# Selection products of the second attention on 48 rows, in pairs over two row tiles, with one buffer of transposed keys

## What is computed

```python
def _L1_attn_ref(x, w_attn, w_proj):   # H = 16 heads of 8 elements, T = 512
    qkv = x @ w_attn
    q = qkv[..., :D].reshape(Bv, Tv, H, HEAD_D).transpose(0, 2, 1, 3)
    k = qkv[..., D:D + HEAD_D]          # one key and one value for all heads
    v = qkv[..., D + HEAD_D:]
    att = jnp.einsum('bhqd,bkd->bhqk', q, k) * scale
    att = jnp.where(causal[None, None, :, :], att, -jnp.inf)
    att = jax.nn.softmax(att, axis=-1)
    y = jnp.einsum('bhqk,bkd->bhqd', att, v)
```

## Times and profile before

| | us |
|---|---|
| median of three runs | 853.83 (848.96 to 860.17) |
| profiled execution, time | 861.02 |
| its span | 859.3 |
| busy: PE, DVE | 681.4, 583.3 |
| busy: ACT, POOL | 349.4, 328.8 |

### The profile page before, as it was taken

The page is one execution under the profiler, slowest core; times in us unless marked ns, Lnnn a source line. Parts: engine busy times, 40 slices in busy tenths (PEclk is TensorE's granted clock), DMA queues, the critical chain, the costliest instruction groups (busy, mean ns, idle before and its releaser), DMA issues. The chain is left out here.

```text
span 859.3 us, 14978 instructions
## 1 busy us (share of the span) xinstructions
PE 681.4 (79%) x4376; PEld 413.4 (48%) x4409; DVE 583.3 (68%) x1923; ACT 349.4 (41%) x748; POOL 328.8 (38%) x430
## 2 busy tenths in 40 slices
PE   1579989984048999999974779898989898898794
PEld 1445666652025788777762224444444444443353
DVE  8378888886921312544357988888889898977373
ACT  0322333304302212222311127666666666666761
POOL 0256656640065636677630003333333332333330
PEclk9999999997558859999995579999999999999996
DMA  9200000000411212222234213020404040300021
GB/s 297 80 1 1 0 1 0 1 1 26 134 40 32 37 19 35 34 40 38 35 77 55 37 22 49 12 57 3 56 4 56 3 57 9 50 4 3 1 62 38
DMA packets 40350, 32.44 MB, mean 38 GB/s; under 512 B 3608, under 2 KB 36936, under 8 KB 40280
## 3 DMA queue, kind: packets, MB, share of 16 engines
q1 hardware_dynamic: 30448, 23.51, 12.6%
q0 software_dynamic: 7840, 6.86, 5.4%
q10 hardware_dynamic: 1992, 1.21, 0.8%
HBM read 13.60 MB, written 8.13 MB: 25 GB/s over the span
## 5 line engine op out<-in xcount | busy, mean ns | idle before, releaser
L1602 ACT ACTIVATE pexp<-wide 128x512 f32<-128x512 f32 (+2 forms) x384 | 183.7, 543 | 118.5 <-PE wide L1791 112.3
L1551 POOL TENSOR_SCALAR_AFFINE_SELECT pexp<-pexp 128x256 f32<-128x256 f32 x256 | 107.3, 422 | 284.1 <-ACT pexp L1602 282.6
L1414 DVE CUSTOM_DVE_ANT_0 masked<-bank,mask_qk 128x384 f32<-128x384 f32 (+3 forms) x356 | 155.2, 480 | 22.0 <-PE bank L1742 20.0
L1791 PE MATMUL wide<-qT,kTe 128*128 128x256 bf16 (+3 forms) x501 | 120.7, 301 | 19.0 <-ACT pexp L1602 8.8
L1070 ACT ACTIVATE hT<-wide,b1T 128x512 f32<-128x512 f32 x64 | 43.5, 687 | 162.8 <-PE wide L1090 134.3
L1742 PE MATMUL bank<-kTm,qT 128*128 128x384 bf16 (+3 forms) x348 | 89.0, 320 | 17.1 <-DVE mx L1414 8.7
L1804 PE MATMUL bank<-pexp,vx 128*32 128x512 f32 (+3 forms) x1024 | 95.5, 445 | 0.8 <-POOL pexp L1551 0.8
L945 POOL DMA_INDIRECT x_dram<-yg,row_u x40 | 63.9, 1596 | 58.0 <-DVE yg L994 49.5
L1414 DVE CUSTOM_DVE_ANT_0 masked<-wide,mask_qk 128x256 f32<-128x256 f32 (+3 forms) x156 | 74.3, 499 | 15.5 <-PE wide L1742 12.9
L938 POOL DMA_INDIRECT x_row<-xln_dram,row_u x64 | 61.8, 965 | 52.8 <-DVE slot_tok L815 33.6
L1099 PE MATMUL bank<-w_sb,hT 128*128 128x128 f32 x512 | 75.4, 292 | 3.2 <-issue 3.2
(11 more groups left out here) (232 smaller groups left out, 1071.8 us busy)
## 6 DMA issues: line engine op xcount, KB each, us to landing
qT<-qp SPq DMA_DIRECT2D x135, 64.0 KB
x_sb<-in_L_attn_x SPq DMA_DIRECT2D x8, 256.0 KB, 6.7
w_sb<-in_L_ffn_w SPq DMA_DIRECT2D x1, 2048.0 KB, 13.1
xln_dram<-rx SPq DMA_DIRECT2D x8, 256.0 KB, 2.3
out_x<-x_sb SPq DMA_DIRECT2D x8, 256.0 KB, 2.3
x_dram<-x_sb SPq DMA_DIRECT2D x5, 256.0 KB, 3.5
x_sb<-x_dram SPq DMA_DIRECT2D x5, 256.0 KB, 3.0
x_row<-xln_dram,row_u POOLq DMA_INDIRECT x64
```

The costliest lines, as they stand in the source:

```text
L1414: ins = nc.vector.tensor_tensor_reduce(out=masked[:, n % 4, at], in0=bank_of(n)[:, at], in1=mask_qk[:, T - w:T], scale=1.0, scalar=LEAST, ...
L1551: nc.gpsimd.affine_select(out=pexp[:, n % 4, :, 0:P], in_=pexp[:, n % 4, :, 0:P], pattern=[[0, 2], [1, P]], compare_op=ALU.is_ge, fill=0.0 ...
L1602: nc.scalar.activation(pexp[:, (2 * step + h // 2) % 4, h % 2:h % 2 + nh, 0:w], psE[m % 3][:, 0:nh * w].rearrange("p (h t) -> p h t", h=nh ...
L1791: ins = nc.tensor.matmul(psE[m % 3][:, hh * w:(hh + 1) * w], kTe[:, par, j * P:(j + 1) * P], qT[:, b % QB, 4 * qd + h + hh, j * P:T], star ...
```

## The change

1. The max products keep the six largest pairs of parts, 48 rows. Heads 0 to 7 have them in rows 0 to 47, heads 8 to 15 in rows 64 to 111; the three remaining pairs lie in other rows (`ROWS_OF_HALF`), and `KEYS_IN_BLOCKS` fills the key slots to fit, with four DVE copies in place of three. The scores products still sum all nine pairs, now over 123 rows (`QR` is 120).
2. `pe_max_pair` makes a unit of a lower and of an upper head together: matmuls on rows 0 to 47 and on rows 64 to 111 alternate, into two banks. It waits for both banks and for the rows of both halves.
3. Units are numbered in pairs, and `PAIRS_IN_STEP` places pairs: the first of a step in place B, the second in D (step 12: C).
4. `kTe` and its copy go; `kTm` has three buffers and the rows of -1 (120 to 122), set once by POOL at the start of the kernel.

```diff
+    BLOCKS = 2 * P // 16 - 1
+    QR = BLOCKS * L
+    LARGE = 6 * L
+    ROWS_OF_HALF = (((0, 3, 5), (1, 4, 6), (2, 7, 14)), ((8, 11, 13), (9, 12, 6), (10, 7, 14)))
+    KEYS_IN_BLOCKS = ((0, 0, 2, 0, 3), (1, 0, 2, 3, 5), (1, 0, 1, 7, 8), (2, 0, 2, 5, 7))
...
-        kTm = sb("kTm", [P, 2, T], BF16)
+        kTm = sb("kTm", [P, QB, T], BF16)
...
-        for h0 in range(0, HEADS, 4):
+        for h0 in range(0, HEADS // 2, 4):
             for k in range(NT):
                 nh = max(1, 4 // (k + 1) if k != 2 else 1)
-                max_units += [(k, h, nh) for h in range(h0, h0 + 4, nh)]
+                for h in range(h0, h0 + 4, nh):
+                    max_units += [(k, h, nh), (k, h + HEADS // 2, nh)]
...
-        IN_STEP = (4, 3, 2, 2, 1, 2, 2, 2, 5, 4, 3, 3, 2, 4, 2, 3)
-        AHEAD = sum(IN_STEP[SHIFT_STEP:])
+        PAIRS_IN_STEP = (2, 2, 1, 1, 1, 1, 1, 0, 2, 2, 2, 1, 1, 1, 2, 2)
+        AHEAD = 2 * sum(PAIRS_IN_STEP[SHIFT_STEP:])
...
-                n = 0 if spot not in spots else IN_STEP[s] // len(spots) + (spots.index(spot) < IN_STEP[s] % len(spots))
+                n = 2 * (spot in spots[:PAIRS_IN_STEP[s]])
...
-            return ops(kx3[:, :, :, n, :], kp[:, n].unsqueeze(2).broadcast_to([P, NT, PARTS, L]))
+            part, g0, ng, lo, hi = KEYS_IN_BLOCKS[n]
+            return ops(kx3[:, :, g0:g0 + ng, lo % 8:lo % 8 + hi - lo, :],
+                       kp[:, part].unsqueeze(2).unsqueeze(2).broadcast_to([P, NT, ng, hi - lo, L]))
...
-        def dve_kTe(dve, b, par):
-            dve.wait_ge(q_kTm.sem, q_kTm.at(b, 1))
-            if b:
-                dve.wait_ge(q_sp.sem, q_sp.at(b - 1, 0))
-            nc.vector.tensor_copy(kTe[0:QR, par, :], kTm[0:QR, par, :]).then_inc(q_kTe.sem, 1)
...
-            nc.vector.memset(vx[:, :, :, :], 0.0)
-            nc.vector.tensor_copy(kTe[64:P, :, :], shift_rows[64:P, :].unsqueeze(2).broadcast_to([64, 2, T])).then_inc(q_init.sem, 1)
+            nc.vector.memset(vx[:, :, :, :], 0.0).then_inc(q_init.sem, 1)
...
-                for j in range(PARTS):
-                    row = (n * PARTS + j) * L
+                for block in ROWS_OF_HALF[half][n]:
+                    row = block * L
...
-        def pe_max_unit(pe, b, n, place):
+        def pe_max_pair(pe, b, n, places):
+
             k, h, nh = max_units[n]
-            pe.wait_ge(q_row[h // 8].sem, q_row[h // 8].at(b, PARTS * PARTS))
+            for half in range(2):
+                pe.wait_ge(q_row[half].sem, q_row[half].at(b, PARTS * PARTS))
             pe.wait_ge(q_kTm.sem, q_kTm.at(b, 1))
             w = P * (k + 1)
             for hh in range(nh):
-                ins = nc.tensor.matmul(place[:, hh * w:(hh + 1) * w], qT[:, b % QB, h + hh, k * P:(k + 1) * P],
-                                       kTm[:, b % 2, 0:w], start=True, stop=True)
-            ins.then_inc(q_smp.sem, 1)
+                for half, place in enumerate(places):
+                    rows = slice(64 * half, 64 * half + LARGE)
+                    ins = nc.tensor.matmul(place[:, hh * w:(hh + 1) * w],
+                                           qT[rows, b % QB, 8 * half + h + hh, k * P:(k + 1) * P],
+                                           kTm[rows, b % QB, 0:w], start=True, stop=True)
+                    if hh == nh - 1:
+                        ins.then_inc(q_smp.sem, 1)
...
+            pool.wait_ge(s_c.sem, s_c.total(16))
+            nc.gpsimd.tensor_copy(kTm[96:P, :, :], const("shift_rows")[96:P, :].unsqueeze(2).broadcast_to([P - 96, QB, T])).then_inc(s_zero.sem, 1)
+            pool.wait_ge(s_zero.sem, s_zero.total(3))
```

More of the change, by code:

```diff
@@ L1229, in build @@
         vx = scratch("vx", [P, 2, NT, 32])
-        kx3 = scratch("kx3", [P, NT, PARTS, PARTS, L], BF16)
-        kTe = scratch("kTe", [P, 2, T], BF16)
+        kx3 = scratch("kx3", [P, NT, 2, 8, L], BF16)
         mx = scratch("mx", [P, NT, HEADS])
@@ L1381, in dve_k_slots @@
             dve.wait_ge(q_kTp.sem, q_kTp.at(b, 0))
-            for n in range(PARTS):
+            for n in range(len(KEYS_IN_BLOCKS)):
                 fill_k_slots(nc.vector.tensor_copy, n).then_inc(q_kx.sem, 1)
@@ L1465, in dve_turn @@
                         dve_divide(dve, b - 1, tail_of(b).divide[s, place])
-                    if middle and s == KTE_STEP and place == "A":
-                        dve_kTe(dve, b + 1, 1 - b % 2)
+                    if middle and s == V_STEP and place == "A":
                         dve_v(dve, b + 1, 1 - b % 2)
@@ L1585, in act_kv, with act_kT @@
                                  ACT.Copy).then_inc(q_kv.sem, 1)
-        def act_kT(act, b, par):
+        def act_kT(act, b):
             act.wait_ge(q_kTp.sem, q_kTp.at(b, 1))
-            act.wait_ge(q_smp.sem, q_smp.at(b - 1, 0))
-            act.wait_ge(q_kTe.sem, q_kTe.at(b - 1, 0))
-            nc.scalar.activation(kTm[0:QR, par, :], psA[:, :].bitcast(BF16)[0:QR, 0:T], ACT.Copy).then_inc(q_kTm.sem, 1)
+            if b >= QB:
+                act.wait_ge(q_sp.sem, q_sp.at(b - QB, NS))
+            nc.scalar.activation(kTm[0:QR, b % QB, :], psA[:, :].bitcast(BF16)[0:QR, 0:T], ACT.Copy).then_inc(q_kTm.sem, 1)
         def act_exp(act, b, step, parts=None):
@@ L1640, in act_turn @@
                 if front and s == KT_STEP:
-                    act_kT(act, b + 2, b % 2)
+                    act_kT(act, b + 2)
         def mqa_act(act):
@@ L1690, in mqa_sync @@
         def mqa_sync(sp):
-            sp.wait_ge(s_zero.sem, s_zero.total(2))
+            sp.wait_ge(s_zero.sem, s_zero.total(3))
             q_rows(sp, 0, 0)
@@ L1759, in pe_max @@
                     pe.wait_ge(q_kTm.sem, q_kTm.at(b + 1, 1))
-                pe_max_unit(pe, b, n, bank[i])
+                if n % 2:
+                    pe_max_pair(pe, b, n - 1, (bank[unit_bank[n - 1]], bank[i]))
         def pe_max_at_start(pe, units):
-            for n in units:
+            for n in units[::2]:
                 if n >= len(psM4):
-                    pe.wait_ge(q_mx.sem, q_mx.at(0, n - len(psM4) + 1))
-                pe_max_unit(pe, 0, n, psM4[n % len(psM4)])
+                    pe.wait_ge(q_mx.sem, q_mx.at(0, n - len(psM4) + 2))
+                pe_max_pair(pe, 0, n, (psM4[n % len(psM4)], psM4[n % len(psM4) + 1]))
         def pe_shift(pe, b, front):
@@ L1790, in pe_scores @@
                 for hh in range(nh):
-                    ins = nc.tensor.matmul(psE[m % 3][:, hh * w:(hh + 1) * w], kTe[:, par, j * P:(j + 1) * P],
-                                           qT[:, b % QB, 4 * qd + h + hh, j * P:T], start=True, stop=True)
+                    ins = nc.tensor.matmul(psE[m % 3][:, hh * w:(hh + 1) * w], kTm[0:QR + PARTS, b % QB, j * P:(j + 1) * P],
+                                           qT[0:QR + PARTS, b % QB, 4 * qd + h + hh, j * P:T], start=True, stop=True)
                 ins.then_inc(q_sp.sem, 1)
@@ L1879, in mqa_pe @@
             pe_kv(pe, 1)
-            pe_max_at_start(pe, range(2 * PER_QUAD, 3 * PER_QUAD))
+            pe_max_at_start(pe, range(2 * PER_QUAD, 3 * PER_QUAD + 1))
             pe_kT(pe, 1)
-            pe_max_at_start(pe, range(3 * PER_QUAD, NM))
+            pe_max_at_start(pe, range(3 * PER_QUAD + 1, NM))
             pe_shift(pe, 0, True)
@@ L1939, in _ @@
         def _(dve):
-            nc.vector.memset(kTm[64:P, :, :], 0.0).then_inc(s_zero.sem, 1)
-            nc.vector.memset(qT[64:P, :, :, :], 0.0).then_inc(s_zero.sem, 1)
+            nc.vector.memset(qT[64:P, :, 0:HEADS // 2, :], 0.0).then_inc(s_zero.sem, 1)
+            nc.vector.memset(qT[0:64, :, HEADS // 2:HEADS, :], 0.0).then_inc(s_zero.sem, 1)
             dve.wait_ge(s_started, LIN)
@@ L1986, in constants @@
         "seqmask": ((n[:, None] % 64) // 8) == np.arange(8)[None, :],
-        "shift_rows": np.where((n >= 72) & (n < 75), -1.0, 0.0)[:, None],
+        "shift_rows": np.where((n >= 120) & (n < 123), -1.0, 0.0)[:, None],
     }
```

18 lines of the change are left out of this document (7 added, 11 removed).

## The result

The changed kernel takes 874.22 us, median of four runs (871.41 to 883.92), against 851.81 for the kernel before on the same chip: ratio 1.0228 [1.0148, 1.0308]. Timed once more beside the experiments it is 875.15 us, ratio 1.0302 [1.0252, 1.0352]. It is slower by two to three per cent, 22.4 and 22.9 us by the medians, where 10.6 us more was forecast: about twice as much.

A forecast was written before the change was run, and what follows sets the result against it. No engine was full; PE and DVE waited for each other through the max products' banks. Terms 5.4 + 1.5 + 4.2 + 0.5 - 1.0 = +10.6 us took the median from 853.8 to 864 us, range 843 to 882.

The forecast's parts named there:

- the net on PE: PE in a steady turn: changes of rows cost 4.4 us, pairs save 2.8, so +1.6 us a turn.
- half of the net is felt: Steady turns and turn 6: PE's idle time swallows half of the net, leaving 0.8 us a turn, +5.4 us in all.
- Steady turns: Second attention: turns of 42 to 43 us expected after the change, from 41.58; under 41 would refute the row-change forecast.
- The start: Sequence 0's first max product waits for both halves' rows, DVE's first maximum comes later: +4.2 us, bounds 2.5 and 4.7.
- Lead-in: Ahead of turn 0, 12 units instead of 11 come before the first scores product: +0.5 us.
- Step 13: First unit behind the transposes of the maxima waits for their copy, DVE idles 0.5 us a turn: +1.5 us, bounds 0 and 3.
- DVE otherwise: DVE per sequence: seven key copies to `kTe` go, a fourth fill is added: -1.0 us.
- The terms taken at nothing: POOL's copy and memsets, `kTm` buffers, ACT's copy on 120 partitions, later row DMAs, turn 7: no cost.
- Row tiles that don't overlap: Rival, chance 0.13: in the turns row changes cost 4.4 us and pairs save nothing; +34.7 us, 888.
- DVE starving between pairs: Rival, chance 0.15: in steps 2 to 6 pairs take both usable banks, DVE waits 2.5 us a turn; +26 us, 879.
- Pairs that relieve PE: Rival, chance 0.25: row changes cost next to nothing and pairs overlap, turns lose 2 to 3 us; 844 or 837.
- the forecast's 0.47: Chance given to the forecast itself, whole kernel: +10.6 us, its own range 856 to 873.

The follow-up runs named there:

- single 48-row units: The new layout with units, order and waits of the kernel before, each max product alone on the 48 rows of its half: 880.1 us, 1.0322.
- the later start: The kernel before, with the first max product of sequence 0 waiting for the rows of both halves: 860.92 us, 1.0115.
- layout only: The kernel before with the new layout and one buffer of transposed keys; units, order and waits as before, singly on 120 rows: 849.91 us, 0.9986.
- the old start: The changed kernel with sequence 0's units singly, lower heads first, each waiting for its own half's rows: 868.91 us, 1.0181.
- both repairs: The changed kernel with sequence 0's units in the old manner and DVE's division ahead of the maxima in the same place: 858.0 us, 1.0083.
- without bank 0: Both repairs, and no unit uses bank 0 in step 13: 862.46 us, 1.0137.
- the earlier scores: Without bank 0, and the first scores of turn 0 ahead of the last two of the six pairs made before it: 863.22 us, 1.0155.

## Why the prediction was right or wrong

**Sign and mechanism of the net on PE.** The forecast rested on pairs whose saving is eaten by changes of rows. That holds: tiles and full rows take the same time within the intervals (875.15 and 875.48). Both terms were off a little. A change costs 0.105 us in each direction, not 0.10 and 0.14: 36 x 0.105 = 3.8 us in a turn, not 4.4. Upper matmuls start less than 0.01 us behind the lower, not 0.07, so pairs save some 4.2 us and not 2.8. The net is some -0.4 us in a turn and not +1.6. The step that failed is the spacing taken from four weight loads in a row: the weight load of the other rows does not show between the starts of a pair. The Trainium skill, TensorE: Matmul & The Clock Gate, Part 3, has some 4 ns between the starts of tiles that run together; the trace agrees as far as it resolves. By its rule this term would have been right. The step "half of the net is felt" held about where it could be tested, 2.9 of 6.4 us on single 48-row units.

**Steady turns.** 42 to 43 us were forecast and 43.0 to 43.3 came, but by another cause: that the length came out so near is luck. I had asked what a pair does to PE's list and to the banks, and not what it does to DVE's: two units in a place double the DVE work that stands ahead of everything written behind `dve_max`. That is the division, for which PE's transposes wait; the prediction had no term for it, which put it at nothing. It was in the code and in the order of the change, and it is the largest single item, 10 us in the median and 8.3 in the second part. With PE's net at -0.4, the forecast's +5.4 us for the turns had no basis; what stood there was a wait that I hadn't counted.

**The start.** Forecast +4.2 us with the bounds 2.5 and 4.7; measured +5.4, outside them, and +4.3 for the wait alone in the kernel before. The mechanism was right, and that nothing takes it back too. Rows of both halves landed 1.1 us later after the change: T0 to ACT's next write of `qp` is 18.9 us in the earlier trace rows and 20.0 above. It is 19.1 in the kernel before with the later start and 19.9 with the layout only, so the later landing comes with the new layout and not with the pairs. The prediction had no term for this, and what in the layout delays the rows is open.

**Lead-in.** Forecast +0.5 for the twelfth unit; from first maximum to first exp it is 41.0 us instead of 39.3 in the changed kernel, and 41.0 with the old start too. With layout only it is 39.8 and with single units on 48 rows 40.0, so about 1.1 us come with the six pairs of sequence 1 ahead of turn 0. The term was mis-sized.

**The first quad.** It costs 2.7 us and stands in no term of the prediction. The busy rows of the changed kernel behind its first exp at 517.86 (the granted clock is the third column from the end):

```profile
519.90:521.90 2.00, 2.00 (x9) 0.44 (x12) 1.04 (x4) 1.79 (x6) 0.81 (x2) 0.50 0.00 0
521.90:523.90 2.00, 1.90 (x12) 0.22 (x4) 0.39 (x1) 0.69 (x3) 0.41 (x1) 0.67 0.00 0
523.90:525.90 2.00, 1.59 (x14) 0.49 (x14) 2.00 (x7) 1.37 (x3) 0.48 (x2) 1.00 0.00 0
```

The granted clock is back at 1.00 about 5 us behind the first exp. In the kernel before, in layout only and with pairs on full rows it is 2.3 to 3.2 us. That fits the pairs on full rows, whose first quad takes 13.40 us against 14.70. It fits the other kernels too: the first quad takes 11.2 us where the clock is back 0.9 us behind the first exp (the later start in the kernel before), 14.0 at 3.9 (both repairs), 14.9 at 5.1 and 16.7 at 8.3 (without bank 0, without and with the earlier scores), 19.7 at 18.9 (single units on 48 rows). That is an order, not a test, and the clock isn't all of it: pairs on full rows have it back after 2.3 us and still need 13.40 us, and layout only has it back after 2.7 and needs 11.72. That rest wasn't taken apart.

**Step 13.** The idle time came out as predicted (0.52 us), its price didn't: taking it away brought nothing. I priced a gap on an engine without asking which wait ends last in that step. PE waits for the transfer of the maxima behind it, and without the gap it waits longer (1.55 us instead of 0.57 in the same turn).

**DVE otherwise.** Forecast -1.0 us; layout only measured 1.2 us less than before by the medians, which its interval [0.9963, 1.0009] does not tell from nothing, and 1.8 us more in the second part. The terms taken at nothing have no cost above 2 us there, but for the later rows under the start.

**Rivals.** Row tiles that don't overlap: excluded. DVE starving between pairs: DVE's waits for max products are 3.0 + 2.2 = 5.2 us in a turn and were 5.1 before; not it, though two small waits for ACT are new (0.7 and 0.6), and though the longest of the 5.2, 1.57 us, does stand in the steps named by that rival. Pairs that relieve PE: its premise on the overlap was right and its sign wrong, since the changes of rows do cost something, 0.105 us where the experts' rows had 0.19. The time itself, 874, lies outside the 856 to 873 that the forecast gave its own mechanism, in the part of the range that was there for the starving rival, and that mechanism is not what brought it there: that 843 to 882 holds it is luck in part. In the chances, 0.07 of the forecast's 0.47 is 0.03 and not 0.05. Sizes: start 5.4, lead-in 1.7 and first quad 2.7 make 9.8 of the 22.0 us; the turns make 11.8, of which the division's place is most (its move took 8.3 off the second part, 7.1 of them in the turns). Both repairs stay 8.8 us behind layout only in the second part. By the marks these lie 1.2 us between first maximum and first exp, 2.3 in the first quad, 3.3 in the turns (2.5 of them in turn 4, with the wait for rows and the lower clock) and 1.9 behind. No run took them apart further, so their causes are read from the trace and not shown.

## What to carry to other kernels

When instructions are grouped to suit one engine, look at what stands behind the group in the list of every engine that serves it: here the group was nearly free on PE and cost 10 us by the order on DVE, through a division of 0.5 us that nobody had moved. Row tiles halve the streaming of narrow products but pay 0.105 us at each change of rows. One pair of up to 512 columns between full-height products saves no more than the two changes cost; by these figures several pairs in a row would win, which no run here tries. And joining work of two halves joins their waits: the first pair starts when the later half is there. Last, look at the granted clock of a turn before putting its length down to a wait.

## What the runs showed of the hardware

- Two matmuls of 48 rows, on rows 0 to 47 and 64 to 111, start at most 0.01 us apart, each with its own weight load (timeline of the changed kernel, 672.97 and 672.98).
- A change between 48-row and full-height bf16 products costs 0.10 to 0.11 us in either direction. The Trainium skill, TensorEngine Tiling (Array Packing), Key Properties, says that a change of mode drains the engine; the trace shows the lost time, which agrees, and not the draining itself.
- On single 48-row units the granted clock stayed at 0.50, the lower level of 1.2 GHz, until some 19 us behind the first exp at 509.12, with PE busy all the time, and rose only there:

```profile
511.00:513.00 2.00, 2.00 (x9) 0.49 (x7) 1.62 (x11) 1.32 (x4) 0.82 (x2) 0.50 0.00 0
...
523.10:525.10 2.00, 2.00 (x5) 0.56 (x5) 0.91 (x3) 1.09 (x2) 0.00 (x0) 0.50 0.00 0
527.00:529.00 2.00, 2.00 (x15) 0.52 (x14) 0.43 (x1) 1.68 (x4) 0.41 (x1) 0.75 0.00 0
```

  With 120-row units in the same order (first exp at 498.40) it had risen within 3 us:

```profile
500.00:502.00 2.00, 2.00 (x16) 1.21 (x17) 1.49 (x11) 1.91 (x5) 0.91 (x3) 0.73 0.00 0
502.00:504.00 2.00, 2.00 (x19) 0.76 (x15) 1.75 (x9) 1.77 (x5) 0.41 (x1) 1.00 0.00 0
```

  Whether the fewer rows hold it down by themselves, or the gaps at the changes do, no run here tells.
- The same clock can fall in turn 7, which has no selection. With both repairs it does for some 7 us, twice as long as in the changed kernel, and turn 7 with the end took 2 us longer. The other three kernels with so long a fall there, all with the old start, also take 56.2 us from the last turn's mark to the end, and the rest 53.4 to 55.2:

```profile
810.60:813.60 3.00, 2.33 (x14) 1.26 (x15) 2.97 (x5) 3.00 (x8) 1.10 (x2) 0.50 0.00 0
813.60:816.60 3.00, 3.00 (x14) 0.65 (x13) 0.24 (x1) 1.69 (x4) 0.81 (x2) 0.50 0.00 0
```
- It can fall inside a steady turn as well, at a wait of PE: the rows of both repairs at 697.20 to 708.00 above, behind 4 us in which PE was busy for 2.40. The turn with it was 2.1 to 2.5 us longer than turns 1 to 3.
